# Transposes of a four-layer graph kernel: from TensorE to block transfers and 32x32 VectorE passes

## What is computed

```python
qkv = (x @ W_qkv).reshape(B, N, HEADS, 3, DIM_HEAD)
dots = jnp.einsum('bhid,bhjd->bhij', q, k) * scale        # masked
attn = jax.nn.softmax(dots, axis=-1) * LA
attn = attn + LG * adj + LD * jnp.exp(-dist)              # dist is adj here
out  = jnp.einsum('bhij,bhjd->bhid', attn, v)
return out @ W_out + b_out
```

## Time and profile before

| what | value |
|---|---|
| median of 2 runs | 1293.49 us |
| profiled execution, span | 1291.5 us |
| busy: TensorE, weight loads | 1247.2 us (97%), 1110.3 us (86%) |
| busy: VectorE, ScalarE, GpSimd | 1068.8 us (83%), 971.6 us (75%), 478.5 us (37%) |
| DMA packets of queue q1 | 42688, 31.47 MB, 8.4% of 16 engines' span |
| HBM read, written | 23.87 MB, 8.39 MB |

### The profile page before, as it was taken

How to read it: one execution, slowest core, us unless ns; L and a number is a source line. 1 busy time by engine, 2 the same in 40 slices (tenths; PEclk the granted TensorE clock), 3 DMA queues, 4 the chain that set the end, 5 groups by cost and what they waited for, 6 DMA issues and landing times.

```text
span 1291.5 us, 32910 instructions
## 1 busy us (share of the span) xinstructions
PE 1247.2 (97%) x9589; PEld 1110.3 (86%) x9589; DVE 1068.8 (83%) x3399; ACT 971.6 (75%) x2806; POOL 478.5 (37%) x1126
## 2 busy tenths in 40 slices
PE   6799999999999999999999999999999999999985
PEld 5688888888888888888898888898888898888874
DVE  3688888888888898888898888888888888888885
ACT  5477877777877777877777787778787777787773
POOL 3233444333443333443333343333343433344432
PEclk9899999999999999999999999999999999999998
DMA  6000100000000000000000100000001000000000
GB/s 214 17 8 21 26 25 25 16 16 18 25 25 25 22 11 17 25 25 25 25 9 17 25 25 25 25 8 19 23 25 25 25 8 23 20 25 25 17 9 9
DMA packets 44293, 32.52 MB, mean 25 GB/s; under 512 B 8176, under 2 KB 43120, under 8 KB 44272
## 3 DMA queue, kind: packets, MB, share of 16 engines
q1 hardware_dynamic: 42688, 31.47, 8.4%
q0 software_dynamic: 176, 0.52, 0.2%
q10 hardware_dynamic: 1408, 0.27, 0.1%
HBM read 23.87 MB, written 8.39 MB: 25 GB/s over the span
## 4 chain that ended last, share of the span: by engine, by line
PE 93%; DVE 3%; ACT 1%; issue 1%; DMA 1%; POOL 0%; DVEq 0%; SPq 0%; POOLq 0%; ACTq 0%
PE PS L405 15%; PE PS L406 15%; PE PS L409 15%; PE PS L494 5%; PE PS L548 5%; PE PS L495 5%; PE PS L498 5%; PE PS L528 4%; PE PS L538 4%; PE PS L584 3%; PE PS L568 2%; PE PS L598 2%; PE PS L520 2%; DVE ysb L1447 1%; PE PS L611 1%; PE PS L604 1%
## 5 line engine op out<-in xcount | busy, mean ns | idle before, releaser
L1722 POOL TENSOR_TENSOR rs<-mv,eps_c 128x1 f32<-128x1 f32 x256 | 61.2, 239 | 582.9 <-DVE mv L1208 581.4
L1726 POOL TENSOR_TENSOR rs<-rs,mhalf 128x1 f32<-128x1 f32 x320 | 176.3, 551 | 25.3
L891 ACT ACTIVATE prob<-PS,neg_max 128x128 f32<-128x128 f32 x512 | 179.7, 416 | 2.0 <-DVE neg_max L1272 2.0
L1285 DVE SCALAR_TENSOR_TENSOR prob<-prob,rl,gate 128x128 f32<-128x128 f32 x512 | 145.6, 347 | 1.5
L494 PE MATMUL PS<-xT_hi,wqk_hi 128*128 128x256 f32 x512 | 141.3, 297 | 0.0
L495 PE MATMUL PS<-xT_hi,wqk_lo 128*128 128x256 f32 x512 | 134.9, 285 | 0.0
L891 ACT ACTIVATION_READ_ACCUMULATOR prob<-PS,neg_max 128x1 f32 x512 | 131.4, 257 | 0.0
L1319 DVE SCALAR_TENSOR_TENSOR hid<-PS,Dn,b_bc 128x512 f32<-128x512 f32 x64 | 48.1, 751 | 85.4 <-PE PS L409 85.4
L498 PE MATMUL PS<-xT_lo,wqk_hi 128*128 128x256 f32 x512 | 103.5, 284 | 0.0
L494 PEld LDWEIGHTS PS<-xT_hi,wqk_hi 128*128 128x128 f32 x512 | 98.2, 192 | 5.3 <-issue 5.0
L495 PEld LDWEIGHTS PS<-xT_hi,wqk_lo 128*128 128x128 f32 x512 | 98.7, 193 | 0.0
(11 more groups left out here) (225 smaller groups left out, 4227.3 us busy)
## 6 DMA issues: line engine op xcount, KB each, us to landing
xin<-in_x_dram SPq DMA_DIRECT2D x32, 256.0 KB, 2.7
out_dram<-xout SPq DMA_DIRECT2D x32, 256.0 KB, 2.2
adj_in<-in_adj_dram SPq DMA_DIRECT2D x32, 128.0 KB, 2.1
wrow<-in_adj_dram SPq DMA_DIRECT2D x32, 128.0 KB, 4.5
wqkv_raw<-in_L_gnn_W_qkv_dram SPq DMA_DIRECT2D x1, 1536.0 KB, 7.6
w_raw<-in_L_gnn_W_dram SPq DMA_DIRECT2D x3, 512.0 KB, 11.4
mask_bc<-in_nodemask_dram SPq DMA_DIRECT2D x32, 32.0 KB, 2.8
wk_raw<-in_L_gnn_Wk_dram SPq DMA_DIRECT2D x3, 256.0 KB, 9.0
```

The costliest lines, as they stand in the source:

```text
L891: last = act.activation(prob[:, t, h, :], PS[:, bank, k * P:(k + 1) * P], ACT.Exp, bias=neg_max[:, t, h:h + 1], accum_out=row_sum[:, t, h: ...
L1285: last = dve.scalar_tensor_tensor(prob[:, t, h, :], prob[:, t, h, :], rl[:, t, h:h + 1], gate[:, t], ALU.mult, ALU.add)
L1726: return pool.tensor_tensor(rs[:, n, g, 1:2], rs[:, n, g, 0:1], mhalf[:], ALU.pow)
```

## The change

Three kinds of transpose leave TensorE. A transpose of 128x128 is made of two halves: a transfer that permutes blocks of 32 columns, and a VectorE transpose that works within each 32x32 block.

- Features: four DMAs per group (`x_block`) load `xblk`, 32 partitions each, in runs of 32 floats (128 bytes). VectorE transposes 128x512 into `xT` (`xT_`), ScalarE copies the high part from it, GpSimd takes the low part (`xlow_`), which TensorE now waits for.
- Adjacency: four DMAs (`adj_block`) load `ablk`, VectorE transposes 128x256 into `adjT`.
- Probabilities: VectorE transposes 128x1024 of `prob` into `probB` (`pT_(t)`), SyncE stores it to a buffer in HBM (512 KB, 4 KB per partition), waits for that store, and issues four loads that bring the blocks into `probT`, again in runs of 128 bytes: 4 x 1024 runs for each graph. `PV_` waits for these loads.
- Normalisation: VectorE keeps heads 0 to 3 (`norm_(t)`), GpSimd does heads 4 to 7 with two passes of 128x512, a multiplication and an addition. `pT_(t)` waits for both.
- Orders: VectorE does `norm_(0)`, `xT_` of group n, `bn1`, `mv1`, `xT2`, `rl_`, `norm_(1)`, `pT_(0)`, `Z_(0)`, `pT_(1)`, `z0_(0)`. GpSimd does `norm_(0)` before `rs1_`, `norm_(1)` and `xlow_` of group n behind them. The adjacency loads (`reload_adj`) are issued behind the probability transfers.

```diff
             def reload(i):
-                sp.wait_ge(pe_xT0, i)
                 sp.wait_ge(pool_resid0, i)
                 sp.dma_start(xin[:], xg[:, bass.ds(i * G, G), :]).then_inc(x_in, 16)
+                sp.wait_ge(dve_xT, i)
+                for k in range(QB):
+                    sp.dma_start(xblk[k * Q:(k + 1) * Q], x_block(i, k)).then_inc(xb_in, 16)
+                sp.wait_ge(dve_adjT, i)
+                for k in range(QB):
+                    sp.dma_start(ablk[k * Q:(k + 1) * Q], adj_block(i, k)).then_inc(ab_in, 16)
...
+            def prob_blocks(i, t):
+                sp.wait_ge(dve_pT, i * G + t + 1)
+                if not isinstance(i, int) or i > 0:
+                    sp.wait_ge(pT_in[t], i * QB * 16)
+                    sp.wait_ge(pe_OT, i * G * 2 - G * 2 + t * 2 + 2)
+                sp.dma_start(pb_dram[t], probB[:, t]).then_inc(pb_out[t], 16)
+                sp.wait_ge(pb_out[t], i * 16 + 16)
+                src = pb_dram[t].rearrange("(a c) h (k r) -> k c h a r", a=QB, r=Q)
+                for k in range(QB):
+                    sp.dma_start(probT[k * Q:(k + 1) * Q, t].rearrange("c h (a r) -> c h a r", r=Q), src[k])\
+                        .then_inc(pT_in[t], 16)
...
             with sp.Fori(0, ITERS - 2) as j:
                 reload(j + 2)
+                prob_blocks(j + 1, 0)
+                prob_blocks(j + 1, 1)
+                reload_adj(j + 2)
                 store_group(j)
...
             def PV_(i, t):
                 pe.wait_ge(act_v, i * G + t + 1)
-                pe.wait_ge(act_PT, i * G + t + 1)
+                pe.wait_ge(pT_in[t], (i + 1) * QB * 16)
...
+                def pT_(t):
+                    dve.wait_ge(dve_attn, i * G + t + 1)
+                    dve.wait_ge(pool_attn, i * G + t + 1)
+                    dve.wait_ge(pb_out[t], i * 16)
+                    dve.transpose(probB[:, t].rearrange("p h n -> p (h n)"), prob[:, t].rearrange("p h n -> p (h n)"))\
+                        .then_inc(dve_pT, 1)
...
+                def norm_(t):
+                    hs = slice(HEADS // 2, HEADS)
+                    pool.wait_ge(dve_rl, i * 2 * G + 2 * t + 2)
+                    pool.wait_ge(pool_gate, i + 1)
+                    step.done(pool.tensor_tensor(prob[:, t, hs], prob[:, t, hs],
+                                                 rl[:, t, hs].unsqueeze(2).to_broadcast([P, HEADS // 2, P]), ALU.mult))
+                    pool.tensor_tensor(prob[:, t, hs], prob[:, t, hs],
+                                       gate[:, t:t + 1].to_broadcast([P, HEADS // 2, P]), ALU.add).then_inc(pool_attn, 1)
```

More of the change, by code:

```diff
@@ L471, in gate_sums @@
                 last.then_inc(set_pe, 1)
[L473 to L485, removed]
             def qk_(i, k):
@@ L719, in group @@
                 if L:
+                    after(pe, act_v, 2, s, 2)
                     qk_(n, 1)
@@ L1277, in rl_ @@
                     dve.wait_ge(act_exp, i * 2 * G + 2 * t + half + 1)
-                    counted[t, half] = step.count(dve.reciprocal(rl[:, t, hs], row_sum[:, t, hs]))
-                def norm_(t, half):
+                    dve.reciprocal(rl[:, t, hs], row_sum[:, t, hs]).then_inc(dve_rl, 1)
+                def norm_(t):
+                    dve.wait_ge(dve_rl, i * 2 * G + 2 * t + 1)
                     dve.wait_ge(pool_gate, i + 1)
-                    step.wait(counted[t, half])
-                    for h in range(half * (HEADS // 2), (half + 1) * (HEADS // 2)):
+                    settle(dve)
+                    for h in range(HEADS // 2):
                         last = dve.scalar_tensor_tensor(prob[:, t, h, :], prob[:, t, h, :], rl[:, t, h:h + 1], gate[:, t],
@@ L1303, in mv0_ @@
                     aggregate(step, counted[t], NORM0, t, dve_mv0)
-                return (step, xT0_, incidence, cnt_, deg_, Be0_, Be_, Dsum_, Dn0_, Dn1_, Dn_, max_, rl_, norm_, OT_, y0_, bn0_,
+                return (step, xT_, incidence, cnt_, deg_, Be0_, Be_, Dsum_, Dn0_, Dn1_, Dn_, max_, rl_, norm_, pT_, OT_, y0_, bn0_,
                         mv0_)
@@ L1504, in group @@
                     rl_(0, 1)
-                    norm_(0, 0)
                 if B:
@@ L1509, in group @@
                 if F:
-                    norm_(0, 1)
+                    norm_(0)
+                if L:
+                    front(n)[1]()
                 if B:
@@ L1520, in group @@
                 if F:
-                    rl_(1, 0)
-                    norm_(1, 0)
+                    norm_(1)
+                    pT_(0)
                 if B:
@@ L1525, in group @@
                 if F:
-                    norm_(1, 1)
+                    pT_(1)
                 if B:
@@ L1628, in first @@
                 rl_(0, 1)
-                norm_(0, 0)
-                norm_(0, 1)
+                norm_(0)
+                rl_(1, 0)
                 rl_(1, 1)
-                rl_(1, 0)
-                norm_(1, 0)
-                norm_(1, 1)
+                norm_(1)
+                pT_(0)
+                pT_(1)
                 centre_w3()
@@ L1780, in group @@
             def group(i, j, n):
-                F, B = i is not None, j is not None
+                F, B, L = i is not None, j is not None, n is not None
                 s = i if F else j + 1 if B else n - 1
                 if F:
-                    fstep, fresid_, gate_, rs0_ = front(i)
+                    fstep, fresid_, _, gate_, norm_, rs0_ = front(i)
                 if B:
@@ L1798, in group @@
                     rsh_(1)
+                if F:
+                    norm_(0)
+                if B:
                     rs1_(0)
                     rs1_(1)
+                if F:
+                    norm_(1)
+                if L:
+                    front(n)[2]()
+                if B:
                     rs2_(0)
@@ L1814, in first @@
             def first():
-                fstep, fresid_, gate_, rs0_ = front(0)
+                fstep, fresid_, xlow_, gate_, norm_, rs0_ = front(0)
                 pool.wait_ge(pool_const, 10)
+                xlow_()
                 pool.wait_ge(ld_vec, 16 * 3)
@@ L1821, in first @@
                 gate_products()
+                norm_(0)
+                norm_(1)
+                front(1)[2]()
                 low()
```

146 lines of the change are left out of this document (73 added, 73 removed).

## The result

The kernel after takes 1600.17 us (median of two runs, 1598.5 to 1601.85) against 1293.49: ratio 1.2369, 95% interval [1.2345, 1.2392]. Its profiled execution has a span of 1596.3 us and a mean granted clock of 0.92.

A forecast was written before the change was run, and what follows sets the result against it. TensorE was taken to bound the 38.49 us turn; less 0.93 gained, plus 8.6 round-trip wait and 1.5 clock gives 47.7. With 31 x 9.2 = 285 and 8 for group 0: 1586 us, likeliest case 1540 to 1675, given range 1520 to 1850.

The forecast's parts named there:

- second place: Last matmul of `T2_(j,1)`, ahead of the `PV_` at 629.60, needs VectorE's `yT_lo`: 0.2 of 0.87 us gained.
- third place: `T3_(j,1)`, whose third matmul needs VectorE's `zb_lo`: it ends 0.3 us earlier, not 0.94.
- first place: `Z_(j,0)`, right behind the transposes, needs ScalarE's copy `xT_hi`: 0.43 of 1.31 us gained.
- The round trip: From the end of `pT_(0)`, store and four loads land at 629.6: TensorE waits 8.6 us at `PV_(i,0)`.
- The rival of dear short runs: Probability loads: a 128-byte run costs 45 ns like a 1-KB packet, loads take 11.5 us, total 1974 us; chance 0.22.
- VectorE's transposes: VectorE passes of 1.22, 0.69 and 0.4 us, 3.5 us a turn; net plus 0.5 us, hidden behind TensorE.
- TensorE's gains: Transposes leaving TensorE gain 0.93 us a turn over three places (ends 0.5 and 3.12).
- The wait at T1: `T1_(j,0)` waits for `al_`, queued behind `pT_(1)`, some 3 us late; hidden if TensorE waits at `PV_(i,0)`, otherwise 2.9 us a turn.
- The clock: TensorE's granted clock falls from 1.00 to 0.50 with the wait at `PV_(i,0)`: 1.5 us a turn (ends 0 and 2.2).
- GpSimd's passes: GpSimd gets five passes of 128x512 at 1.30 us, 6.5 us of its 24 idle ones.
- Graph 1: Its loads land at 637.5, when TensorE comes to `PV_(i,1)`: no second wait.
- Group 0: One round-trip wait of about 8 us, added to the 31 turns.

The follow-up runs named there:

- the run with the adjacency alone: The kernel before with only the adjacency transposed by block loads and VectorE, x and probabilities staying on TensorE: 1294.95 us, ratio 1.001.
- the late `pT_(1)` run: The changed kernel with VectorE's transpose of graph 1 moved down, from ahead of z0 to behind the second z2: 1608.62 us, ratio 1.2433.
- the run without that wait: The changed kernel with PV_ reading probB from VectorE without waiting for the loads, all transfers still issued: 1480.65 us, ratio 1.1447.
- filling the waits: The changed kernel with 30 extra 128x512 matmuls a turn on TensorE, 12 ahead of the second si and 18 behind it: 1555.36 us, ratio 1.2025.
- the run with the early `pT_(0)`: The changed kernel with VectorE's transpose of graph 0 moved up to right behind norm_(0): 1492.56 us, ratio 1.1536.

## Why the prediction was right, by its steps

Forecast 1586 us, measured 1600.17, inside the narrow range of 1540 to 1675. Forecast turn 47.7, measured 47.82. TensorE's places of the two traces are laid over each other at the start of `h_`, 602.36 before and 699.48 after, 97.12 apart. The lines of the kernel before for it:

```profile
602.36 0.40 PE L405 MATMUL PS<-w1t_hi,axT_hi 128*128 128x512 f32 x1
...
618.37 0.85 PE L409 MATMUL PS<-wk_hi,xT_lo 128*128 128x260 f32 x4
```

The account of a turn, in the time of the kernel before:

| step | forecast | measured |
|---|---|---|
| TensorE would arrive at `PV_(i,0)` without waits at `si_` | 621.0 | 621.5 |
| store issued | 620.2 | 621.0 |
| first load issued | 623.4 | 623.6 |
| loads landed, `PV_(i,0)` starts | 629.6 | 629.05 |
| wait at `si_(1)` and `PV_(i,0)` | +8.6 | +7.6 |
| from there to `PV_(i,1)` (clock, second place) | +1.3 | +1.4 |
| from `PV_(i,1)` to `h_` (third place) | -0.3 | +0.3 |
| first place | -0.43 | 0 |
| turn | +9.2 | +9.3 |

The mechanism was right. That the turn came within 0.1 us is luck in part: the wait was 1.0 us shorter than forecast, and two gains of TensorE, in the first and in the third place, 1.0 us together, did not come.

- *The round trip* was the right mechanism, with errors that partly cancel. `pT_(0)` ended 0.9 us later than forecast, since VectorE has `xT_` (0.69 us) and a longer `norm_(0)` ahead of it. From the issue of the store to that of the first load it took 2.65 us, not 3.2: the store lands in 2.6 us, where 2.9 were forecast. The loads took 5.4 us from the first issue, not 6.2: a 128-byte packet costs 0.434 x 16 x 3.2 / 1732 = 12.8 ns by the DMA view, below even the lower end of the estimate, 14.3, where 18 was taken. Against it the issues took 0.70 us each, not 0.46. What makes them long is not shown; the loads of `xblk`, with half as many runs, took 0.76 us each. The rival of dear short runs, 45 ns each, falls with this. The 512-byte minimum of the Trainium skill, "DMA: Bandwidth & Descriptors", section "Specifications", that stood beside it holds in one sense and not in the other: 128 bytes in 12.8 ns are fewer bytes in a time than 512 in 26.3, but the time of a packet does not rise below 512 bytes, where 256 took 14.3. At this size it is the number of packets that counts.
- *VectorE's transposes* took 1.24, 0.70 and 0.44 us against 1.22, 0.69 and 0.4, as the groups by line show:

```profile
L1300 DVE STREAM_TRANSPOSE probB<-prob 128x1024 f32<-128x1024 f32 x64 | 79.3, 1240 | 47.7 <-issue 47.7
L1215 DVE STREAM_TRANSPOSE xT<-xblk 128x512 f32<-128x512 f32 x32 | 22.3, 697 | 1.5 <-DMA xblk<-in_x_dram 1.5
L1222 DVE STREAM_TRANSPOSE adjT<-ablk 128x256 f32<-128x256 f32 x32 | 14.1, 440 | 0.0
```

  The estimate from the Trainium skill's "VectorE: DVE Perf Modes", section "The three transpose paths", 2.5 us for eight, was twice too high; the measurement decides.
- *TensorE's gains* failed: -0.93 was forecast. In the first place the high passes did start at 713.73 - 97.12 = 616.6 as worked out, but the low passes wait for VectorE's `xT_lo`, which ends at 715.36, and start at 715.42 - 97.12 = 618.30, where they had started at 618.37. VectorE has `xT_` and a stretched norm ahead of it. The working looked at ScalarE's copy alone. In the third place the matmul that needs `zb_lo` still waits for it, 0.38 us, and `ax_` behind it now waits 0.19 us for `x1t` of ScalarE. In the run with the adjacency alone the third place is worth nothing; with x as well, and no GpSimd pass, 0.26 us was the whole gain. The second place was not tried alone.
- *The wait at T1* was forecast for VectorE held by `pT_(1)`, "some 3 us late". It came, 2.79 us, but at `si_(1)`, which needs VectorE's `sji` first. That it is hidden behind the trip was right (the late `pT_(1)` run), and so was its price of 2.9 us where TensorE does not wait for the trip: 2.77 in the run without that wait. The expectation of that run had this step; what it left out was the clock.
- *The clock*: 1.5 us a turn forecast, 1.45 measured by filling the waits. It is not a fixed price: behind 2.77 us of waiting, in the run that does not wait for the trip, it was 2.4.
- *GpSimd's passes* were counted as free for VectorE. This step was wrong. With the normalisation and the low part on GpSimd but no trip, a turn is 39.60, not below 38.49. Of these 1.1 us, 0.74 come with x, adjacency and GpSimd's `xT_lo`, and disappear when that pass is taken away (38.23); the other 0.37 come with its half of the normalisation and the new place of `norm_(0)`, which no run separates. In the changed kernel it shows as `norm_(0)` at 1.66 us.
- *Graph 1*: no wait at `PV_(i,1)`, as forecast.
- *Group 0*: 8 us were forecast beside 31 turns. 304.8 us of span less 31 x 9.3 leaves 16.5, twice as much. Its wait at `PV_(0,0)` is 15.0 us, where 0.3 stood before. The first store of the loop is 5.5 us late with x and the adjacency alone and no GpSimd pass, so part of it comes with these; the rest was not taken apart.

By runs, the 306.7 us are: 119.5 the wait for the transfer beyond `si_(1)`, net of the clock; 44.8 the clock, by filling; 41.2 what stays with the probabilities on TensorE; and 101.2 left over, in which the wait at `si_(1)`, 2.8 x 31 = 87, is the largest. The last is by subtraction, group 0 is in it, and the split assumes that the parts add, which the clock does only roughly.

## What to carry to other kernels

A round trip through memory in a steady loop costs the part of its length, here 8.2 us from the end of `pT_(0)` to the landing, that the work between its source and its use in the written order doesn't cover. Starting it 3.4 us earlier was worth 108 us, halving its loads 31; where nothing waited for it, removing all its traffic was worth nothing. Before work is moved off an engine, check for each place whether that engine waits there for another input; of the 1.4 us of features and adjacency taken from TensorE a turn, 0.26 came out of it. GpSimd as a helper for VectorE is free only where VectorE isn't doing two-input instructions on SBUF at that time.

## What was not expected of the hardware

VectorE instructions with two tensor inputs in SBUF took about 1.0 us longer beside a GpSimd pass of 128x512 that takes 1.4: 0.29 became 1.25 us, 1.14 became 2.17, 2.18 became 3.22. Beside the rest of a pass that had begun before, 1.14 became 1.66. A transpose with one input, 719.57 beside GpSimd's pass at 719.43, took 1.25 us, as alone. This agrees with the Trainium skill, "SBUF — State Buffer", section "SBUF: two separate sides", by which VectorE with two SBUF inputs and GpSimd share a port pair that one of them holds for a whole instruction. The prediction left it out.

The clock: it fell behind 2.77 us of waiting as it did behind 7.3. In the run with the early `pT_(0)`, and 2.77, 1.28 and 0.78 us of waiting, the mean was 0.952; with the waits filled 0.987.
